# Attention and feed-forward on one core: products with V two cycles at a time, masked maxima over whole heads

## The reference

```
q = x @ Wq                        # 32 heads of 16
k, v = split(x @ Wkv)             # 8 groups, each shared by 4 heads
scores = q k^T, causal: key > query -> -inf
weights = softmax(scores / sqrt(16))
x1 = layernorm(x + (weights @ v) @ Wo + bo)
out = layernorm(x1 + x1 @ W^T + bias + sum_n lora_n(x1))
```

## Time and profile before

| | |
|---|---|
| median of 3 runs | 386.68 us (385.4 to 390.87) |
| profiled execution | 384.55 us, span 382.7 us |
| TensorE busy | 346.6 us, 91% of the span |
| VectorE busy | 289.5 us, 76% |
| ScalarE busy | 209.7 us, 55% |
| GpSimd busy | 108.3 us, 28% |
| mean granted clock of TensorE | 0.985 |

### The profile page before, as it was taken

How to read it: one execution, slowest core, us unless ns; L and a number is a source line. 1 busy time by engine, 2 the same in 40 slices (tenths; PEclk the granted TensorE clock), 3 DMA queues, 4 the chain that set the end, 5 groups by cost and what they waited for, 6 DMA issues and landing times.

```text
span 382.7 us, 6579 instructions
## 1 busy us (share of the span) xinstructions
PE 346.6 (91%) x2172; PEld 167.1 (44%) x2173; DVE 289.5 (76%) x1037; ACT 209.7 (55%) x398; POOL 108.3 (28%) x193
## 2 busy tenths in 40 slices
PE   6789689799997999999999989999999999989992
PEld 3666454444542333343423344244342443328871
DVE  3449766788887999997699877998879984307985
ACT  4372236556763666865567736667467566771110
POOL 1382033344433453523030130210211203230341
PEclk9999999999996999999999999999999999999997
DMA  7859991313111021001001010000000000000002
GB/s 233 246 147 276 213 214 49 84 45 97 33 43 33 12 69 40 21 3 42 2 29 43 1 43 2 27 3 1 3 0 29 2 3 1 19 11 2 0 28 82
DMA packets 20769, 21.33 MB, mean 56 GB/s; under 512 B 6080, under 2 KB 16256, under 8 KB 20736
## 3 DMA queue, kind: packets, MB, share of 16 engines
q1 hardware_dynamic: 20736, 20.92, 20.1%
HBM read 14.68 MB, written 6.03 MB: 54 GB/s over the span
## 4 chain that ended last, share of the span: by engine, by line
PE 54%; DVE 24%; ACT 5%; SPq 5%; issue 5%; POOL 4%; DMA 1%; POOLq 0%; DVEq 0%; ACTq 0%
PE PS L1077 13%; PE PS L942 13%; PE PS L914 11%; PE PS L1098 10%; DVE MX L693 5%; DVE MX L698 4%; DVE scrap L701 4%; ACT PB L646 3%; SPq L430 2%; PE PS L1004 2%; DVE stats L785 2%; PE PS L1012 2%; DVE TC L795 1%; DMA QS<-NMR 1%; SPq L399 1%
## 5 line engine op out<-in xcount | busy, mean ns | idle before, releaser
L646 ACT ACTIVATE PB<-PS 128x512 f32<-128x512 f32 (+1 forms) x304 | 157.0, 582 | 86.7 <-PE PS L1098 85.8
L914 PE MATMUL PS<-KS,QS 96*128 96x512 bf16 (+3 forms) x384 | 110.8, 332 | 14.6 <-DVE MX L701 11.1
L1098 PE MATMUL PS<-QS,KS 99*128 99x512 bf16 (+3 forms) x384 | 120.3, 331 | 1.1 <-DMA QS<-NMR 0.5
L542 POOL TENSOR_SCALAR_AFFINE_SELECT PB<-PB 128x256 f32<-128x256 f32 x128 | 51.8, 410 | 184.1 <-ACT PB L646 183.6
L1077 PE MATMUL PS<-PB,VX 128*32 128x512 f32 (+3 forms) x768 | 82.9, 504 | 1.2 <-POOL PB L542 1.2
L693 DVE TENSOR_REDUCE MX<-PS 128x1 f32<-128x512 f32 x128 | 80.7, 681 | 1.9 <-PE PS L914 1.6
L698 DVE TENSOR_REDUCE MX<-PS 128x1 f32<-128x384 f32 (+2 forms) x160 | 75.5, 472 | 7.7 <-PE PS L914 7.5
L701 DVE CUSTOM_DVE_ANT_0 scrap<-PS,mask 128x128 f32<-128x128 f32 x256 | 66.2, 281 | 2.5 <-PE PS L914 2.5
L914 PEld LDWEIGHTS PS<-KS,QS 96*128 96x128 bf16 x384 | 34.6, 98 | 71.5 <-DVE MX L701 28.2
L1098 PEld LDWEIGHTS PS<-QS,KS 99*128 99x128 bf16 x384 | 36.5, 99 | 40.6 <-ACT PB L646 20.8
L942 PE MATMUL PS<-XT,WQ 128*128 128x512 f32 x144 | 40.1, 413 | 4.8 <-DVE WQ L846 3.2
(11 more groups left out here) (72 smaller groups left out, 267.7 us busy)
## 6 DMA issues: line engine op xcount, KB each, us to landing
scr_q<-parts SPq DMA_DIRECT2D x8, 384.0 KB, 3.2
QS<-scr_q SPq DMA_DIRECT2D x16, 192.0 KB, 3.0
X<-in_L_attn_x_dram SPq DMA_DIRECT2D x8, 256.0 KB, 6.6
QS<-scr_q SPq DMA_DIRECT2D x16, 128.0 KB, 3.0
out_dram<-TC SPq DMA_DIRECT2D x8, 256.0 KB, 2.0
RAW<-in_L_attn_Wq_dram SPq DMA_DIRECT2D x1, 1024.0 KB, 8.4
QS<-scr_q SPq DMA_DIRECT2D x16, 64.0 KB, 3.1
RAW<-in_L_attn_Wo_dram SPq DMA_DIRECT2D x1, 1024.0 KB, 6.6
```

The lines of the kernel that those rows point to most:

```text
L542: nc.gpsimd.affine_select(out=blk, in_=blk, compare_op=ALU.is_ge, fill=0.0, base=0, pattern=[[0, 2], [1, P]], channel_multiplier=-1)\
L646: nc.scalar.activation(PB[:, cyc % NP_BUF, heads[0]:heads[-1] + 1, d * P:HT], PS[:, score_bank(e), 0:len(heads) * (HT - d * P)] .rearrange ...
L914: last = nc.tensor.matmul(PS[:, n % MAX_BANKS, k * width:(k + 1) * width], QS[0:ROWS, u % SLOTS, j, qb * P:(qb + 1) * P], KS[0:ROWS, g, k0 ...
L1098: last = nc.tensor.matmul(PS[:, score_bank(e), place * width:(place + 1) * width], KS[0:NROW, u % G, kb * P:(kb + 1) * P], QS[0:NROW, u % ...
```

## The change

The products with V are no longer issued after every cycle. After an even cycle, TensorE issues those of the two cycles before it, one after the other; after an odd cycle it issues none. The last two cycles' products stand after the loop.

In the own chunks one tensor_tensor_reduce per head now goes over all (qb + 1) x 128 columns. The mask is therefore 512 wide, zero in its first 384 columns, with the triangle in its last 128, and in 16 bits; a head uses its last (qb + 1) x 128 columns. The tensor_reduce over the columns before the diagonal block is gone, and so is one of the three columns of MX. The values written beside the maximum go to two buffers of 512 in 16 bits, by the chunk's parity, and an own chunk first waits until the chunk before the previous one is read. chunk_cost is adjusted to the new instructions.

```diff
--- before.py
+++ after.py
@@ -72,7 +72,7 @@
         _, qb, own, heads = ch
         if not own:
             return 65 + HT
-        return len(heads) * (65 + P) + (65 + len(heads) * qb * P if qb else 0)
+        return len(heads) * (80 + (qb + 1) * P)
 
     COST = [0]
     for ch in CHUNKS:
@@ -238,11 +238,11 @@
         bias_bc = sb("bias_bc", [P, D])
         ident = sb("ident", [P, P])
         ident_bf = sb("ident_bf", [P, P], BF16)
-        mask = sb("mask", [P, P])
+        mask = sb("mask", [P, HT], BF16)
         Z = sb("Z", [P, HT], BF16)
-        scrap = sb("scrap", [P, 2 * REP, P])
+        scrap = sb("scrap", [P, 2, HT], BF16)
         coef = sb("coef", [P, N_LORA])
-        MX = sb("MX", [P, 2, TB, REP, 3])
+        MX = sb("MX", [P, 2, TB, REP, 2])
         NM = sb("NM", [P, 2, TB, REP])
         NM2 = sb("NM2", [P, 2, TB, REP])
         NMP = sb("NMP", [P, 2, TB, NPART, REP], BF16)
@@ -476,8 +476,8 @@
             constant(nc.gpsimd.affine_select(out=ident[:, :], in_=ident[:, :], compare_op=ALU.not_equal, fill=1.0,
                                              base=0, pattern=[[-1, P]], channel_multiplier=1), 1)
             link(nc.gpsimd.memset(mask[:, :], 0.0))
-            constant(nc.gpsimd.affine_select(out=mask[:, :], in_=mask[:, :], compare_op=ALU.is_ge, fill=LOWEST,
-                                             base=0, pattern=[[-1, P]], channel_multiplier=1), 2)
+            constant(nc.gpsimd.affine_select(out=mask[:, HT - P:HT], in_=mask[:, HT - P:HT], compare_op=ALU.is_ge,
+                                             fill=LOWEST, base=0, pattern=[[-1, P]], channel_multiplier=1), 2)
             constant(nc.gpsimd.memset(MX[:, :, :, :], LOWEST), 3)
             constant(nc.gpsimd.tensor_copy(ident_bf[:, :], ident[:, :]), 4)
             link(nc.gpsimd.memset(minus_half[:, :], -0.5))
@@ -680,8 +680,6 @@
                 ins.then_inc(dve_step, 1)
                 dve.wait_ge(dve_step, step[0])
 
-            turn = [0]
-
             def chunk_max(n):
 
                 u, qb, own, heads = CHUNKS[n]
@@ -694,13 +692,13 @@
                     return
                 width = (qb + 1) * P
                 bank = bank[:, 0:len(heads) * width].rearrange("p (j t) -> p j t", t=width)
-                if qb:
-                    nc.vector.tensor_reduce(part[:, j0:j1, 1:2], bank[:, :, 0:qb * P], AX, ALU.max)
+                if n >= 2:
+                    dve.wait_ge(max_read, n - 1)
                 for j in heads:
-                    turn[0] = (turn[0] + 1) % (2 * REP)
                     last = nc.vector.tensor_tensor_reduce(
-                        out=scrap[:, turn[0], :], in0=bank[:, j - j0, qb * P:width], in1=mask[:, :], scale=1.0,
-                        scalar=LOWEST, op0=ALU.add, op1=ALU.max, accum_out=part[:, j, 2:3])
+                        out=scrap[:, n % 2, (j - j0) * width:(j - j0 + 1) * width], in0=bank[:, j - j0, :],
+                        in1=mask[:, HT - width:HT], scale=1.0, scalar=LOWEST, op0=ALU.add, op1=ALU.max,
+                        accum_out=part[:, j, 1:2])
                 last.then_inc(max_read, 1)
                 if n + 1 == UNIT_CHUNKS[u + 1]:
                     finish_maxima(u)
@@ -1113,11 +1111,13 @@
                     head_scores(cyc, j)
                     if j % 2:
                         filler(cyc, j // 2)
-                if cyc:
+                if cyc and cyc % 2 == 0:
+                    accumulate(cyc - 2)
                     accumulate(cyc - 1)
                 filler(cyc, 2)
                 if cyc in ROWS_AT:
                     turn_maxima(ROWS_AT[cyc])
+            accumulate(NCYC - 2)
             accumulate(NCYC - 1)
```

## The result

The changed kernel took 394.25 us, the median of 4 runs (390.68 to 396.78), against 387.64 for the kernel before in 4 runs (385.40 to 390.87): a ratio of 1.0145, with a 95% interval of 1.0083 to 1.0207. It is slower, by somewhere between 0.8 and 2.1%, where 380.3 us was forecast. Its profiled execution took 394.02 us, with a span of 392.3.

The account below looks back on a forecast made before the run. TensorE was taken as the bound, VectorE close behind. 384.55 - 6.5 (merged products) - 2.9 (masked maxima) + 3 (what pairs take away) = 378.15 us profiled, 380.3 us median; range 372 to 389.5.

Parts of the forecast that it names:

- What the merging takes away: Paired products with V leave VectorE idle during double lots; about seven full pairs lose; +3 us, bounds 0 and +14.
- Slower: Rival: double lots starve VectorE's queue and maxima bound the second half; 398 us, chance 0.11.
- Merging the products: TensorE's products with V: one way out and in saved at 47 pairs, 0.23 us each, 10.8 us; -6.5 us taken.
- free joint: Between a pair's two lots on TensorE: cost could be 0 to 0.23 us, taken as 0.
- Only what lies on the path counts ... -6.5 us: Products with V: chain share 0.60 of their busy time, times 10.8 us saved; bounds 0 and -10.8.
- Where VectorE has slack this is free: VectorE's idleness of 0.6 to 0.7 us per pair costs nothing except in full stretches, such as 140 to 160 us.
- the idleness: VectorE at double lots: at most three chunks, 1.8 us, behind, so idle some 0.6 to 0.7 us per pair.
- Other waits keep their distance ... as many lots of products as before, or one more or less, 1 us: TensorE's waits for turned maxima, a unit's first scores and MISC steps keep nearly the same work between; no cost charged.
- Masked maxima: VectorE's own chunks: 512-column head takes 0.61 instead of 0.68 us, 11.2 us less work; -2.9 us, bounds 0 and -11.2.
- The rival of a lost rate: VectorE's masked instruction runs at half rate over 512 columns, adding 51 us of work; 415 us, chance 0.02.
- The base, 386.68 us: Median of the kernel before's three timed runs; profiled execution 384.55 us, result shifted by the 2.1 us between.
- one more fall of the clock: Within the slower rival: a TensorE stall in a burst lowers the granted clock, losing 3.4 us of full speed.

Follow-up runs that it names:

- narrow_pairs: New maxima with single lots, except that the lots of 256 and 128 columns are issued in pairs; 6.0 us slower than the new maxima alone.
- split_pair: Changed kernel with the two lots of an even cycle issued apart, the first after the second head; 1.0158 of the kernel before.
- the relieved kernels: New maxima, single lots against pairs, with columns left out of VectorE's maxima (in one couple also ScalarE's exponentials); pairs cost 4.6, 4.7 and 6.0 us.
- both_again: The changed kernel, unaltered, measured again beside the follow-up kernels; 394.10 us.

## Why the prediction was wrong

**The direction.** Forecast was -1.65%, measured +1.45%. The mechanism that decided was written down, as the step "What the merging takes away" and as the rival "Slower", but it was priced at +3 us and given a chance of 0.11. Measured, the pairs cost +8.1 us net at equal clock and +10.6 in the medians, where the sum had -6.5 + 3 for them. That the time of the rival "Slower", 398 us, came near the measured 394.25 is in part luck: it has +11 us from the queue in units 8 to 15, where at the full clock 2.6 were measured, and nothing in the first four units.

**Merging the products.** The term's size on the array was right: 0.23 us per pair was forecast with a free joint, and with 1.85 us for 16 products it is 2 x (0.09 + 0.99) - (0.09 + 1.85) = 0.22. Its estimate of two rounds of 0.427 us per lot holds too: in the double lot of the changed kernel the first of four rounds starts at 162.3 and the last at 163.6, so 0.43 us each, twice the 0.216 us that 512 columns in 16 bits take, and the second lot adds 1.85 - 0.99 = 0.86 us. L1075's busy time fell by 8.0 us, 10.8 were forecast in all. What failed is the step "Only what lies on the path counts ... -6.5 us". The chain's share says how much of the lots lay on the path while they hid something else. It does not say that taking time out of them leaves the rest where it is.

**What the merging takes away.** This is the step that failed. It gave +3 us against the -6.5, and the pairs cost 8.1 us net. Its first error is "Where VectorE has slack this is free": the slack was read from averages (168.7 of 202 us), and the queue needs it within each burst. Relieving VectorE turned the pairs' cost after unit 3 from 3.8 us to a gain of 2.1, at the full clock. Its second is the idleness. It took VectorE to be three chunks behind when a double lot begins, and in the pair shown it had 0.85 us of work left and stood idle for 1.48 us. (The sum as written, 1.94 + 0.4 - 1.8, is 0.54, not 0.6 to 0.7; and seven pairs that each lose 0.35 and miss a gain of 0.14 and 0.06 make 3.9 us, not 3.) Its third is that it looked at the length of the double lot alone. narrow_pairs shows that short double lots cost too, and split_pair that the cost stays without any: it is the missing lot in the other cycle that uncovers VectorE's waits. The sentence "Other waits keep their distance ... as many lots of products as before, or one more or less, 1 us" saw it and passed over it: one lot less is what turned 0.43 us of waiting into 1.10 at the place shown. And it charged almost nothing for the first half, some 1 us for the part of the stretch from 140 us that lies there; the first half's pairs cost 5.2 us, 2.9 of them from unit 0 to 3, where it had charged none.

**Masked maxima.** Right in the rate and the direction. 0.61 us per head of 512 columns was forecast and 0.60 to 0.61 measured (167.65 to 168.26), VectorE's busy time fell by 9.1 us of 11.2 forecast, and -2.9 us was forecast for the whole; measured were -4.8 and -3.7 us in the medians, -1.8 and -1.3 at equal clock, so the forecast size lies between the two readings. The rival of a lost rate fell.

**The clock.** The base, 386.68 us, was a little too good against medians of 386.9 to 389.1. The profiled execution of the kernel before (384.55 us, clock 0.985) was among the fastest of its kind; the kernel's runs average 0.971 to 0.974. I added the 2.1 us between it and the median without asking what they were made of. And I had priced one more fall of the clock only as an accident of a rival, where the kernels with double lots beside chunk maxima all ran at less clock than those with the new maxima and single lots: it is some 2.5 us of the 10.6, and most of the 4.7 and 6.0 us that the pairs still cost in the relieved kernels.

**What stays open.** Why the pairs cost 2.9 us from unit 0 to 3, and still 3.2 when VectorE's maxima there are relieved, is only suggested by rows at one place (the filler's step before the maxima in VectorE's queue); moving those fillers was not tried. Nor was a fourth bank for the chunks, which would test the depth of the queue directly: the eight banks of the kernel's PS are all taken (three for chunks, three for scores, one for the products with V, one for the fillers).

The version to keep is the new maxima with single lots: 0.9878 and 0.9942 of the kernel before in two sets, and 2.7% faster than the whole change in the first.

## What to carry to other kernels

A block of matmuls that needs nothing from the other engines is not only cost: here it was also the time in which they emptied their queues. Before joining two such blocks, look at the stretch that loses one, and ask for every queue how deep it is in microseconds (banks times time per bank) against the longer stretch and against the longer block; averages of busy time don't tell. When two kernels are compared within 2%, multiply each run's time by its granted clock before looking for causes, and do the same with stretches of a trace: it cut 6.0 us between two unit ends to 2.6.

## What the runs showed of the hardware

The same kernel's mean granted clock scattered between 0.965 and 0.985 from run to run on one core, and its time with it: 391.35 us at 0.965 and 384.38 at 0.985 for the kernel before. Over all 97 runs of it, on four chips, the times lie between 382.5 and 391.4 us and their products with the clock between 375.8 and 379.9, about half the spread; the product's mean was within about 0.2 us in all five sets. Where the clock falls varies too: in two executions of the changed kernel it was 0.50 (both_again) and 1.00 (the first one) from 30 to 32 us. The two runs at 0.965 and 0.985 differ by 1.8%.

Column strips joined without a gap: 16 matmuls in four strips took 1.85 us in one go, where two separate lots of 8 took 0.99 each, with 0.09 before each by the prediction's reading of the earlier trace rows.
